# The query projection of a perceiver layer moved from a program block of its own into the block of attention, chunk by chunk of x

## What is computed

```python
x = x + xattn(layernorm(x), ctx_768, w_q, w_kv, w_out, b_out)   # 16 heads of 64, 1601 keys of 192 channels
x = x + attn(layernorm(x), time_decay, time_first, mixes, Wk, Wv, Wr, Wo, bo)
x = x + ffn(layernorm(x), w1, b1, w2, b2)
```

## Time and profile before

| what | value |
|---|---|
| time, median of 3 runs | 2396.36 us (2393.26 to 2397.3) |
| the profiled execution: its time, its span | 2396.41 us, 2394.6 us |
| PE busy | 2296.1 us (96%) |
| DVE, ACT, POOL busy | 1834.8, 1545.8, 1603.1 us |
| mean granted clock of PE | 0.993 of full |
| DMA | 438.93 MB, mean 183 GB/s |

### The profile page before, as it was taken

How to read it: one execution, slowest core, us unless ns; L and a number is a source line. 1 busy time by engine, 2 the same in 40 slices (tenths; PEclk the granted TensorE clock), 3 DMA queues, 4 the chain that set the end, 5 groups by cost and what they waited for, 6 DMA issues and landing times.

```text
span 2394.6 us, 44090 instructions
## 1 busy us (share of the span) xinstructions
PE 2296.1 (96%) x13696; PEld 2099.9 (88%) x13696; DVE 1834.8 (77%) x3670; ACT 1545.8 (65%) x2690; POOL 1603.1 (67%) x798
## 2 busy tenths in 40 slices
PE   4968999999999999999999999999999999989899
PEld 3647998999999999999999999999999998878788
DVE  7767777777777777777777777777777777779884
ACT  4655666666666676766666766676666666555444
POOL 2006787888888888888888888888888886421111
PEclk9989999999999999999999999999999999999999
DMA  5867888888888888888888888888888886886000
GB/s 156 238 201 168 196 195 194 197 198 199 201 201 200 202 200 199 199 197 199 199 200 200 200 201 200 202 201 199 201 199 199 200 198 162 210 198 172 14 10 27
DMA packets 384766, 438.93 MB, mean 183 GB/s; under 512 B 81856, under 2 KB 355648, under 8 KB 384704
## 3 DMA queue, kind: packets, MB, share of 16 engines
q1 hardware_dynamic: 368880, 427.23, 75.4%
q10 hardware_dynamic: 15824, 10.91, 1.9%
HBM read 167.42 MB, written 52.43 MB: 92 GB/s over the span
## 4 chain that ended last, share of the span: by engine, by line
PE 49%; POOL 21%; issue 12%; DVE 5%; SPq 4%; ACT 1%; DMA 0%; ACTq 0%; POOLq 0%; DVEq 0%
PE p_scores L1462 20%; PE p_acc L1478 13%; POOL p_pt_lo L771 11%; PE p_acc L1480 6%; SPq L655 3%; POOL p_nat L798 3%; POOL p_q_lo L783 3%; POOL p_ct_lo L779 2%; PE p_scores L1582 2%; POOL p_ct_hi L790 2%; PE p_cols L1524 2%; PE p_scores L1628 2%; PE p_cols L1615 2%; PE p_scores L1540 1%; PE p_acc L1482 1%
## 5 line engine op out<-in xcount | busy, mean ns | idle before, releaser
L771 POOL TENSOR_TENSOR p_pt_lo<-p_landed,p_pt_hi 128x768 fp32r<-128x768 f32 x504 | 991.5, 1989 | 320.7 <-ACT p_pt_hi L913 320.7
L1478 PE MATMUL p_acc<-p_nat,p_pt_hi 128*128 128x384 f32 x3024 | 888.1, 361 | 8.9 <-POOL p_pt_lo L771 7.7
L1480 PE MATMUL p_acc<-p_nat,p_pt_lo 128*128 128x192 f32 x3024 | 758.9, 251 | 0.0
L1462 PE MATMUL p_scores<-p_ct_hi,p_q_hi 128*128 128x512 f32 (+2 forms) x2048 | 705.4, 348 | 26.6 <-DVE p_ct_hi L1401 13.8
L949 ACT ACTIVATE p_prob<-p_scores,p_negmax 128x800 f32<-128x800 f32 (+1 forms) x512 | 471.4, 926 | 399.3 <-DVE p_negmax L1213 399.2
L1462 PE MATMUL p_scores<-p_ct_hi,p_q_lo 128*128 128x512 f32 (+2 forms) x2048 | 704.6, 347 | 0.0
L1478 PEld LDWEIGHTS p_acc<-p_nat,p_pt_hi 128*128 128x128 f32 x3024 | 568.4, 188 | 16.8 <-POOL p_pt_lo L771 8.8
L1480 PEld LDWEIGHTS p_acc<-p_nat,p_pt_lo 128*128 128x128 f32 x3024 | 577.9, 191 | 0.0
L913 ACT ACTIVATE p_pt_hi<-p_landed 128x768 fp32r<-128x768 f32 x504 | 398.5, 838 | 163.1 <-PE p_acc L1482 123.8
L1462 PEld LDWEIGHTS p_scores<-p_ct_hi,p_q_hi 128*128 128x128 f32 x2048 | 390.2, 191 | 72.6 <-issue 14.2
L1221 DVE STREAM_TRANSPOSE turned<-p_prob 128x1536 f32<-128x1536 f32 x256 | 452.7, 1768 | 0.0
(11 more groups left out here) (228 smaller groups left out, 3117.3 us busy)
## 6 DMA issues: line engine op xcount, KB each, us to landing
p_landed<-turned SPq DMA_DIRECT2D x2032, 104.0 KB, 2.3
resid<-in_ctx SPq DMA_DIRECT2D x128, 288.0 KB, 4.9
o_scratch<-resid SPq DMA_DIRECT2D x256, 96.0 KB, 2.7
qk_scratch<-p_out_a SPq DMA_DIRECT2D x16, 1024.0 KB, 4.6
p_stage<-qk_scratch SPq DMA_DIRECT2D x31, 512.0 KB, 3.9
p_stage<-qk_scratch SPq DMA_DIRECT2D x62, 256.0 KB, 4.3
p_stage<-in_ctxT SPq DMA_DIRECT2D x31, 401.0 KB, 4.6
p_stage<-in_ctxT SPq DMA_DIRECT2D x62, 200.5 KB, 5.5
```

The source lines that it names most:

```text
L771: nc.gpsimd.tensor_tensor(pt_lo[:, t0:t1, :, :], by_tile(slot, t0, t1), bits(pt_hi[:, t0:t1, :, :]), ALU.subtract).then_inc(pt_lo_done, 1)
L1462: last = nc.tensor.matmul(scores[:, S0 + lo:S0 + hi], w, x, start=m == 0, stop=m == len(terms) - 1)
L1478: nc.tensor.matmul(acc[k % 2][:, 0:2 * DC], pt_hi[:, t, :, :].rearrange("p i x -> p (i x)"), x[:, t, :], start=t == 0, stop=False, skip_gr ...
L1480: nc.tensor.matmul(acc[k % 2][:, 0:DC], pt_lo[:, t, :, :].rearrange("p i x -> p (i x)"), x[:, t, 0:DC], start=False, stop=False, skip_grou ...
```

## The change

`write_queries` is gone. Its work stands at the head of the second block, unrolled (before, chunks 1 to 3 were a hardware loop):

- x is loaded in four parts, w_q in two and w_k in four. They are split in parts.
- Chunk 0 is normalised by DVE ahead of the pairs. Chunks 1 to 3 are treated among the pairs of the chunk before: statistics on DVE at j = 0 and 1, root on ACT at j = 2, inverse on DVE and normalisation **on ACT** at j = 3, the two T sets at j = 5 and 7.
- A store follows every pair, in pieces of 512 B, and a buffer is reused after 4 pairs.
- Batch 0's high parts are made by ACT among pairs of chunks 1 to 3, and its low parts by POOL instead of DVE.
- Q's PSUM banks and T's are now those of the scores, and W's those of `acc` and `cols`.

```diff
-    write_queries(nc, e["x"], ...)
-    attend_and_finish(nc, ...)
+    whole_layer(nc, e["w_q"], e["wkT"], ...)
 @block.sync
+            load_tokens(0); load_query_weights(0); load_key_weights(0); load_query_weights(1)
+            for i in range(1, WKP):
+                load_key_weights(i)
+            for c in range(1, NC):
+                load_tokens(c)
...
+            for g in range(GP):
+                store_queries(g)
+                if g == HP + 1:
+                    for done in qk_stored:
+                        sp.wait_ge(done, 2 * 32)
+                    sp.dma_start(first_q[:, 0, :], qk_dram[0, 0:P, :]).then_inc(first_q_in, 16)
...
+                if g == (NC - 1) * HP:
+                    sp.wait_ge(xp_ready, NC * KB)
+                    for dst, src in raw_pieces(raw, ctx_in, 0):
+                        sp.dma_start(dst, src).then_inc(first_raw_in, 16)
...
+            for done in qk_stored:
+                sp.wait_ge(done, GP // SLOTS * 32)
             passes(sp, body)
 @block.gpsimd
+            query_weights_lo(0); key_weights_lo(0); query_weights_lo(1)
+            for i in range(1, WKP):
+                key_weights_lo(i)
...
+            for h in range(2):
+                first_context_lo(h)
+            for k in range(KB):
+                first_queries_lo(k)
+            for h in range(2):
+                first_rows_lo(h)
 @block.scalar
+            def x_normalised(c):
+                act.wait_ge(x_step, (c + 1) * XLN)
+                for t in range(c * CTT, (c + 1) * CTT):
+                    nc.scalar.activation(xt[:, t, :], xt[:, t, :], ACT.Identity, bias=x_std[:, 4, t:t + 1],
+                                         scale=x_std[:, 3, t:t + 1]).then_inc(x_normal, 1)
...
+            def first_rows(h):
+                t0, t1 = THALF[h]
+                act.wait_ge(first_raw_in, 16 * PIECES)
+                act.wait_ge(wk_lo_done, WKP)
+                nc.scalar.activation(nat[0][:, t0:t1, 0:DC], raw[:, t0:t1, :], ACT.Copy).then_inc(nat_hi_done, 1)
+            query_weights(0); x_roots(0); key_weights(0); x_hi(0); x_hi(1); query_weights(1)
+            for g in range(GP):
+                c, j = divmod(g, HP)
+                stack_high(g)
+                if g > 0:
+                    evacuate_act(g - 1)
+                if c == 0 and j in (0, 1, 2):
+                    key_weights(j + 1)
+                if c + 1 < NC:
+                    if j == 2:
+                        x_roots(c + 1)
+                    if j == 3:
+                        x_normalised(c + 1)
+                    if j in (5, 7):
+                        x_hi(KB * (c + 1) + (j - 5) // 2)
+                if c == 1 and j in (0, 1):
+                    first_context(0, j)
...
+                if c == NC - 1 and j in (3, 5):
+                    first_rows((j - 3) // 2)
 @block.vector
+            x_statistics(0, range(CTT)); x_inverse(0); x_normalised(0); x_lo(0); x_lo(1)
+            for g in range(GP):
+                c, j = divmod(g, HP)
+                stack_low(g)
+                if g > 0:
+                    evacuate_dve(g - 1)
+                if c + 1 < NC:
+                    if j in (0, 1):
+                        x_statistics(c + 1, (2 * j, 2 * j + 1))
+                    if j == 3:
+                        x_inverse(c + 1)
+                    if j in (5, 7):
+                        x_lo(KB * (c + 1) + (j - 5) // 2)
 @block.tensor
+                if j == 0:
+                    pe.wait_ge(xp_lo, (c + 1) * KB)
...
+            x_turned(0); x_turned(1); queries(0)
+            for g in range(GP):
+                c, j = divmod(g, HP)
+                if c + 1 < NC and j in (5, 7):
+                    x_turned(KB * (c + 1) + (j - 5) // 2)
+                if g + 1 < GP:
+                    queries(g + 1)
+                with_keys(g)
```

More of the change, by code:

```diff
@@ new lines, in evacuate_act, with first_context @@
+            def evacuate_act(g):
+                buf_a, buf_b = staged[g % SLOTS]
+                for r in range(2):
+                    act.wait_ge(qk_ready, 2 * g + r + 1)
+                    if g >= SLOTS and r == 0:
+                        act.wait_ge(qk_stored[g % SLOTS], g // SLOTS * 32)
+                    dst, from_bank = (buf_b, bp[r]) if r else (buf_a, ap[r])
+                    nc.scalar.activation(dst[:, :, r, :], batches(from_bank[:, :]), ACT.Copy).then_inc(evac_act, 1)
+            def first_context(part, h):
+                lo, hi = CHALF[h]
+                if part == 0:
+                    act.wait_ge(first_a_in, 16)
+                    nc.scalar.activation(ct_hi[0][:, 0, lo:hi], first_a[:, lo:hi], ACT.Copy).then_inc(ct_a_hi_done, 1)
+                else:
+                    act.wait_ge(first_b_in, 32)
+                    nc.scalar.activation(ct_hi[0][:, 1, lo:hi], first_b[:, lo:hi], ACT.Copy).then_inc(ct_b_hi_done, 1)
@@ new lines, in queries @@
+            def queries(g):
+                c, j = divmod(g, HP)
+                if c == 0 and j in (0, HP // 2):
+                    pe.wait_ge(wq_lo_done, 1 if j == 0 else 2)
+                if j == 0:
+                    pe.wait_ge(xp_lo, (c + 1) * KB)
+                if g >= 2:
+                    pe.wait_ge(stack_lo, g - 1)
+                cols_of = slice(c % 2 * CT, (c % 2 + 1) * CT)
+                terms = [(w, xv, k) for k in range(KB) for w, xv in ((wq_hi, xT_hi), (wq_lo, xT_hi), (wq_hi, xT_lo))]
+                for n, (w, xv, k) in enumerate(terms):
+                    last = nc.tensor.matmul(qp[g % 2], w[:, k, j * P:(j + 1) * P], xv[:, k, cols_of], start=n == 0, stop=n == len(terms) - 1)
+                last.then_inc(q_ready, 1)
@@ new lines, in with_keys @@
+            def with_keys(g):
+                c, j = divmod(g, HP)
+                pe.wait_ge(stack_lo, g + 1)
+                if c == 0 and j % 2 == 0:
+                    pe.wait_ge(wk_lo_done, j // 2 + 1)
+                for r in range(2):
+                    h, q = 2 * j + r, stack[g % 2][:, r, :]
+                    if g > 0:
+                        pe.wait_ge(evac_act, 2 * (g - 1) + r + 1)
+                        pe.wait_ge(evac_dve, 2 * (g - 1) + r + 1)
+                    for n, w in enumerate((wks_hi, wks_lo)):
+                        nc.tensor.matmul(ap[r][:, :], w[:, h, 0:P], q, start=n == 0, stop=n == 1)
+                    for n, w in enumerate((wks_hi, wks_lo)):
+                        last = nc.tensor.matmul(bp[r][:, :], w[:, h, P:DC], q, start=n == 0, stop=n == 1)
+                    last.then_inc(qk_ready, 1)
```

466 lines of the change are left out of this document (200 added, 266 removed).

## The result

The changed kernel takes 2438.2 us (median of 4 runs, 2436.66 to 2440.84) and the kernel before 2396.83 (4 runs): ratio 1.0171, with a 95% interval of 1.0159 to 1.0183. It is 41 us slower. The forecast was 2393, in a range of 2382 to 2402.

A forecast was written before the change was run, and what follows sets the result against it. PE, 96% busy, was taken to bound the kernel, so only an earlier start of attention could win. Terms: 15.9 + 13.6 - 10.2 - 7.2 - 6 - 2.6 = 3.5 us less, so 2393, range 2382 to 2402.

The forecast's parts named there:

- if the steps after the seam differ: Attention steps after the first stage: a difference there would make the prediction wrong; no size or chance given.
- Term 1: Start of the kernel: first Q at 17.3 us instead of 33.24, 15.9 us earlier.
- Terms 3 and 4: Pairs of the first stage: normalisation on ACT, 3 times, loses 10.2 us; T right ahead of its Q, 3 times, 7.2.
- Term 5: ACT at g = 27 waits for batch 0's raw rows, so SH(28) starts late: 6 us lost, bounds 3.5 and 8.5.
- Term 6: Small losses among the pairs: DVE statistics, ACT copies, one operation held by POOL: 2.6 us lost.
- Term 2: Passage from last W to attention: scores follow at once, 13.96 us won; second step 9.95 behind the first; net 13.6 earlier.
- The last W: End of the first stage: last W ends near 160 us; outside 153 to 168 the prediction is wrong.
- The store rival: First-stage pairs: half-size stores bound them, ACT and DVE wait for `qk_stored`, 29 us more, 2422 us; chance 0.1.

The follow-up runs named there:

- 64 memsets: Changed kernel with 64 one-column memsets added at the head of DVE's program, where it idles: 2402.01 us, ratio 1.0012 to the kernel before.
- 8 and 16 memsets: Changed kernel with 8 or 16 one-column memsets added at the head of DVE's program, one run each: 2407.59 us and 2407.24 us.

## Why the prediction was wrong

**The step that failed** is the one in the first paragraph, "nothing after the first 200 us can be won by this change except that everything starts earlier", and with it the sum, which takes the loop over the batches as the same loop. Its instructions are the same, but its place in DVE's code is not, and that costs 36 to 38 us of the 41. The text named "if the steps after the seam differ" as what would make it wrong; I gave it no price and no chance. Its other sign came true as well: the last W ended at 169.6, outside 153 to 168. The listing of both programs had the numbers: 392 and 446 instructions ahead, 28 packets for 3,498 instructions. What was not in the trace of before is that a fourth block costs anything, so no row could have given the price.

The Trainium skill has a rule for it (Runtime: NRT & Kernel Launch, "Instruction fetch mechanics"): a taken branch whose target is outside the two pages held forces a fetch of the target's page before execution goes on. The trace agrees in kind, with 2.8 us a branch. It differs in size: the page gives blocks of 16 KiB, or 256 instructions, and here the packets of DVE's queue are 8.2 KB and the loss comes back after 128.

**The rest of the sum** was 6 to 11 us off. The forecast was 3.5 less. With 64 memsets 2.9 more were measured (0.0012 x 2397), which is inside the range; the single runs with 8 and 16 memsets (2407.6 and 2407.2) are outside it. In the trace of the changed kernel the second step starts at 181.44 and not 173.98, 7.5 later, where the sum has 3.5 earlier. Those 11 us are terms that were mis-sized, below.

- *Term 1* (first Q at 17.3): 17.55. Right, and by the path that was forecast: the quarter of x lands at 4.88, and one operation of DVE's inverse takes 1.72 us and ends at 12.13, where POOL's split of w_k ends (10.32 + 1.80).
- *Terms 3 and 4* (10.2 + 7.2 = 17.4): each stall is where and why it was forecast, 2.7 to 3.0 at j = 3 and 3.0 at j = 7, where the sum had 3.4 and 2.4; that the two errors cancel is luck. Taking both away gives 22.3 against the changed kernel and 17.3 against the one with the memsets. What was left out is the clock: three pairs behind the stalls took 5.3, and TensorE's matmuls 0.63 there. It is the 4.9 between 17.4 and 22.3.
- *Term 5* (6, bounds 3.5 to 8.5): 8.0. ACT's wait of 5.73 is the forecast's; the pair behind it took 5.74 and not 3.7.
- *Term 6* (2.6): with the stalls of terms 3 to 5 taken away, the pairs still take 114.2 us from the first W to the last, 4.5 more than in the kernel before (38.87 to 148.53, 109.7). No run splits them.
- *Term 2*: no gap behind the last W, right. The prediction reads PE's gap of before as 13.96 from 150.45; by the earlier trace rows the last W ended at 150.61 and the gap is 13.80, which changes nothing. The second step came 11.84 behind the first and not 9.95. The load went out 2.53 after the last W as forecast (172.13), its split began 0.7 later than forecast, and the table load of 1.28 was missed: in the kernel before it lay in a wait.
- *The last W* ended at 169.6 and not near 160: 4.9 by the clock, 2.0 by the raw rows, 1.9 by term 6 and 0.3 by the start.
- *The store rival* (2422): false. ACT and DVE never waited for `qk_stored`; the narrower stores landed in 4.2 us (median of both forms).

## What to carry to other kernels

Before a hardware loop, count the instructions ahead of it and in it on each engine: whatever lengthens the code ahead, an unrolled stage above all, can lay the loop over one more block, and the price returns at every branch back (here 1.8 to 3.9 us each, 13 times). Its sign is idle time that ends in "issue" at the first instruction of a round, with instruction packets where there were none; a few empty instructions in idle time move the loop, and are worth a run before an edit is judged, since the place can hide a gain as large as the edit's. And a stall of TensorE of 3 us can cost 4.6 (the pairs g = 4 and 5 took 11.67 us, and 7.09 without the stall), since the pair behind it may run at the lower clock.

## What the runs showed of the hardware

- The loss on DVE has a period of 128 instructions (446 and 574 ahead of the loop are bad, 510 is good), and the packets of its queue hold about as many (8.2 KB). At a good place DVE waits 0.3 us at a branch back. At a bad one it waits 3.0 to 5.8, five packets are fetched, and a round gets 1.8 to 3.9 us longer. Which five they are, the trace doesn't say.
- A place 14 instructions away from another bad one cost 29 us more (2455.9, one run, against 2427.1), with as many packets.
- Behind a stall of 3 us the granted clock fell, in chunk 0 of the changed kernel (the next pair took 5.32 us) and not in the same place of the same order with 64 memsets (3.78). In five profiled executions that differ only in the memsets (none, 8, 16, 64, 128) the first stage took 139.4 to 144.9 us from the first W to the last.
